# Cross-attention and FP4 feed-forward on one core: key and value projections as five one-pass products of two-part operands, key and query parts buffered for half the heads

## The chip, the cores and the metric

The kernel runs on one core of a Trainium2 chip. The metric is the device time of one launch in microseconds. The engines are TensorE (PE), VectorE (DVE), ScalarE (ACT), GpSimd (Pool) and SyncE (SP), which here only issues DMAs.

## The reference

For each of 16 batch elements, x is 512 x 256 and the context is 1601 x 192, all in float32:

```
Q = layernorm(x) @ Wq;  K = ctx @ Wk;  V = ctx @ Wv      # 16 heads of 16
P = softmax(Q K^T / 4);  x = x + (P V) @ Wo + bo
a = fp4(layernorm(x)); g = a @ fp4(w_gate)^T; u = a @ fp4(w_up)^T      # 704 wide
x = x + fp4(silu(g) * u) @ fp4(w_down)^T
```

fp4 scales blocks of 16 values by their largest magnitude, rounds to eight levels and scales back.

## The kernel before

The work of one batch element is a batch. Its 16 heads are taken in four groups of four (phases). In a group, the 1601 keys are taken in 13 tiles of 128, one step for each: four scores (keys x 512 queries, one per head), an exp of each on ACT, and a weighted sum of the four heads' values on PE. The scores have two PSUM banks in turn, so PE is at most two scores ahead of ACT.

Each projected key and query is split into three bf16 parts (`k_parts`, `q_parts`), and six pairs of parts are stacked along the contraction axis (96 rows of `k_stack`, `q_stack`), so that one bf16 matmul gives a float32-like score. The stack of one head is filled by 12 DMAs on SP's queue ("stack", g, j): six copy 16 rows of `q_parts`, six 16 rows of `k_parts`. `k_parts` and `q_parts` hold both halves of the heads (half 0: groups 0 and 1, half 1: groups 2 and 3). Three more rows carry the negated maximum of each query. It comes from the pieces: while one group is scored, PE computes the scores of the next group with the queries on the partitions, as 64 x 4 matmuls of 400 columns per batch (64 in each group), and DVE takes the maximum of each piece (L829, L1097). Then "max_parts" on DVE splits the maximum in three, "maxima" transposes it, and DMAs put it in `q_stack`.

Around this lies all other work, as events: layernorm, transposes and projections of the next batch ("ln1_*", "x_T", "ctx_T", "q_proj", "k_proj", "v_proj"), and what follows attention for the batch before, in four quarters of 128 rows ("heads_T" to "down"). A batch has 104 half-steps, 26 for each group; tables at the top (POST_AT, PRE_AT, MAX_AT, HEADS_OUT_AT, LN1) say at which half-step an event stands. `sequence` merges scores, pieces, weighted sums and rounds (PE's part of an event) into one order by estimated PE cycles; pieces go only into half-steps 0 to 21 of a group. PE, ACT and DVE follow this order, Pool and SP the order of the events. The engines take their work in that order. Rounds use two PSUM banks in turn; the engine that empties a bank counts `work_drained`, and PE waits for it.

A key or query round is two float32 products on PE (L729, L737). ACT copies it as bf16 part 0 (L867, L871), DVE subtracts that part from the bank into `rest` and frees the bank (L1003), and Pool makes parts 1 and 2 from `rest` (L1177, L1179). A context round is four transposes and a copy by ACT (L865). Values are two float32 products for each key tile (L745) and a copy by ACT (L878). At the start of a group SP issues the stacks of heads 1 to 3 of the next group, once the scores of the group before are done (they had the same slots), and the stack of head 0 of the group after it; in group 0 also x and the context of the next batch. A batch "start" (prologue) comes before the first batch; "first" prepares the feed-forward weights in the place of the post-processing, "last" prepares no batch, "tail" finishes the last one.

## Time and profile before

| | us |
|---|---|
| median of 3 runs (3776.65 to 3781.04) | 3777.42 |
| profiled execution | 3777.43 |
| its span, first to last instruction | 3775.6 |
| PE busy | 3599.6 |
| DVE busy | 2984.2 |
| ACT busy | 2242.8 |
| Pool busy | 871.0 |

The mean granted TensorE clock is 0.992. Busy time is a mean over stages with different limits. A matmul's record reaches to the end of its result, so consecutive records overlap: what one costs is read from start to start. A float32 matmul of this kernel shows as two records. The chain is the work that ended last, followed back to what released it. "SPq" rows are issues of DMAs on SP's queue.

### The profile page before, as it was taken

Reading aid. Unit: us, or ns where it says so; the run is one execution under the profiler, and the core shown is the slowest. Engines: PE = TensorE matmul, PEld = TensorE weight load, DVE = VectorE, ACT = ScalarE, POOL = GpSimd, SP = SyncE. Lnnn points to the kernel's source line nnn. Section 1 sums busy time; section 2 is a strip of 40 time slices with the busy share of each in tenths; the row PEclk is TensorE's granted clock in tenths of the full one; section 3 lists DMA queues with packets and bytes.
Section 4 is the critical chain, followed back from the end, with each engine's and each line's share of the span. In section 5 each row is a group of like instructions: output and inputs, shape, how many; then the busy total and the mean of one; then the engine's idle time right before and its main releaser. Section 6 shows DMA issues by size and latency. Waiting matters only on the chain.

```text
span 3775.6 us, 57225 instructions
## 1 busy us (share of the span) xinstructions
PE 3599.6 (95%) x19654; PEld 1643.5 (44%) x19654; DVE 2984.2 (79%) x6641; ACT 2242.8 (59%) x4350; POOL 871.0 (23%) x920
## 2 busy tenths in 40 slices
...
GB/s 67 51 50 53 24 59 34 36 54 34 51 36 42 41 42 49 29 48 39 39 55 24 60 33 35 53 36 50 35 43 40 44 49 28 49 39 38 38 22 7
DMA packets 148034, 156.44 MB, mean 41 GB/s; under 512 B 58129, under 2 KB 118818, under 8 KB 147746
## 3 DMA queue, kind: packets, MB, share of 16 engines
...
q14 instruction: 130, 1.06, 0.1%
...
## 4 chain that ended last, share of the span: by engine, by line
PE 75%; DVE 15%; ACT 4%; DMA 2%; issue 2%; SPq 1%; POOL 0%; POOLq 0%; ACTq 0%
PE out_ps L815 17%; PE score_ps L804 16%; PE piece_ps L829 16%; PE work L770 8%; DVE piece_max L1097 6%; PE work L745 5%; PE work L737 5%; PE work L780 4%; ACT probs L914 4%; DMA x_in<-in_x 2%; PE work L760 1%; PE work L724 1%; PE work L754 1%; PE work L729 1%; DVE neg_parts L1012 1%
## 5 line engine op out<-in xcount | busy, mean ns | idle before, releaser
L1097 DVE TENSOR_REDUCE piece_max<-piece_ps 128x1 f32<-128x400 f32 (+1 forms) x4096 | 2134.0, 566 | 537.3 <-PE piece_ps L829 519.5
L914 ACT ACTIVATE probs<-score_ps 128x512 f32<-128x512 f32 (+1 forms) x3328 | 1876.3, 598 | 1021.7 <-PE score_ps L804 1016.6
L829 PE MATMUL piece_ps<-k_stack,q_stack 96*128 96x400 bf16 (+1 forms) x4096 | 1282.7, 336 | 67.1 <-DVE piece_max L1097 59.5
L804 PE MATMUL score_ps<-q_stack,k_stack 99*128 99x512 bf16 (+1 forms) x3328 | 1258.5, 385 | 48.7 <-ACT probs L914 14.4
L815 PE MATMUL out_ps<-probs,v_ones 128*17 128x512 f32 x6656 | 878.0, 599 | 2.1 <-ACT probs L914 1.0
L804 PEld LDWEIGHTS score_ps<-q_stack,k_stack 99*128 99x128 bf16 (+1 forms) x3328 | 324.4, 98 | 879.7 <-ACT probs L914 642.3
L829 PEld LDWEIGHTS piece_ps<-k_stack,q_stack 96*128 96x128 bf16 x4096 | 396.8, 98 | 649.9 <-DVE piece_max L1097 430.6
L1152 POOL TENSOR_TENSOR h<-h,h_grid 128x704 f32<-128x704 f32 (+1 forms) x68 | 111.3, 1637 | 1081.7 <-DVE h_grid L966 1081.7
L770 PE MATMUL work<-wgu_T,xq_T 128*128 128x256 f32 (+1 forms) x1440 | 345.3, 361 | 0.4 <-ACT xq_T L886 0.4
L770 PEld LDWEIGHTS work<-wgu_T,xq_T 128*128 128x128 f32 x1440 | 258.8, 189 | 48.6 <-ACT xq_T L886 3.4
L815 PEld LDWEIGHTS out_ps<-probs,v_ones 128*17 128x17 f32 x6656 | 110.3, 95 | 279.7 <-issue 235.1
L737 PE MATMUL work<-ctx_T,wk_sb 128*128 128x512 f32 (+1 forms) x512 | 217.9, 513 | 0.0
L745 PE MATMUL work<-wv_sb,ctx_T 128*128 128x256 f32 (+1 forms) x832 | 215.1, 380 | 0.1
L780 PE MATMUL work<-wd_T,h_T 128*128 128x256 f32 x744 | 188.2, 378 | 0.8 <-ACT h_T L904 0.8
L1177 POOL TENSOR_TENSOR k_parts<-rest,zero 128x512 bf16<-128x512 f32 (+1 forms) x128 | 110.5, 863 | 332.5 <-DVE rest L1003 332.5
L892 ACT ACTIVATE tanh_g<-work 128x256 f32<-128x256 f32 (+1 forms) x192 | 70.4, 367 | 189.9 <-PE work L770 185.9
L745 PEld LDWEIGHTS work<-wv_sb,ctx_T 128*128 128x128 f32 (+1 forms) x832 | 151.1, 185 | 36.7 <-ACT v_ones L878 4.8
L780 PEld LDWEIGHTS work<-wd_T,h_T 128*128 128x128 f32 x744 | 137.9, 189 | 26.8 <-ACT h_T L902 1.0
L1188 POOL TENSOR_TENSOR rstd<-mean_var,eps 128x1 f32<-128x1 f32 x64 | 12.4, 193 | 475.4 <-DVE mean_var L1040 474.2
L1152 POOL TENSOR_TENSOR xq<-xq,xq_grid 128x256 f32<-128x256 f32 x60 | 43.4, 724 | 334.0 <-DVE xq_grid L966 334.0
L1179 POOL TENSOR_TENSOR k_parts<-rest,k_parts 128x512 bf16<-128x512 f32 (+1 forms) x128 | 117.7, 920 | 10.0
L871 ACT CAST k_parts<-work 128x512 bf16<-128x512 f32 (+1 forms) x128 | 63.0, 495 | 93.7 <-PE work L737 93.7
...
## 6 DMA issues: line engine op xcount, KB each, us to landing
k_stack<-k_parts SPq DMA_DIRECT2D x1536, 50.0 KB, 2.2
q_stack<-q_parts SPq DMA_DIRECT2D x1536, 16.0 KB, 1.8
...
q_stack<-neg_rows SPq DMA_DIRECT2D x192, 4.0 KB, 1.7
...
```

The costliest lines, as they stand in the source:

```text
L737: last = pe.matmul(work[:, 0:w], wk_sb[:, part, e * P:(e + 1) * P], ctx_T[:, part, a:a + w], start=(part == 0), stop=(part == 1))
L745: last = pe.matmul(work[0:r, u * D:(u + 1) * D], ctx_T[:, k, a:a + r], wv_sb[:, k, :], start=(k == 0), stop=(k == 1))
L770: last = pe.matmul(work[:, u * GW:u * GW + w], quarter(kind, t).xq_T[:, k, :], wgu_T[:, k, u, j * GW:j * GW + w], start=(k == 0), stop=(k ...
L780: last = pe.matmul(work[:, 0:D], quarter(kind, event[1]).h_T[:, c, :], wd_T[:, c, :], start=(c == 0), stop=(c == FT - 1))
L804: pe.matmul(score_ps[0:r, n % SCORE_RING, :], k_stack[:, par, slot(g, j), m * P:m * P + r], q_stack[:, par, slot(g, j), :], start=True, st ...
L815: last = pe.matmul(out_ps[32 * j:32 * j + V1, :], v_ones[0:r, batch[1] % 2, m, PER_GROUP * g + j, :], probs[0:r, step % 2, j, :], start=(m ...
L829: pe.matmul(piece_ps[:, n % PIECE_RING, 0:hi - lo], q_stack[0:SROWS, par, slot(g, j), t * P:(t + 1) * P], k_stack[0:SROWS, par, slot(g, j) ...
L914: act.activation(probs[0:r, step % 2, j, :], score_ps[0:r, (PER_GROUP * m + j) % SCORE_RING, :], ACT.Exp, scale=SCORE_SCALE).then_inc(prob ...
L1097: dve.tensor_reduce(piece_max[:, row, c:c + 1], piece_ps[:, n % PIECE_RING, 0:piece_at[c + 1] - piece_at[c]], AX_X, ALU.max).then_inc(piec ...
L1152: pool.tensor_tensor(src, src, grid, ALU.add).then_inc(done, 1)
L1177: pool.tensor_tensor(parts[:, half, 1, a:a + w], rest[:, n % 2, 0:w], zero[:].broadcast_to([P, w]), ALU.add).then_inc(split_step, 1)
L1179: pool.tensor_tensor(parts[:, half, 2, a:a + w], rest[:, n % 2, 0:w], parts[:, half, 1, a:a + w], ALU.subtract).then_inc(split_step, 1)
```

## The change

- `wk_sb`, `wv_sb` and `ctx_T` become float32r in two parts, high (a copy, rounded) and low (the float32 value less the high part). The contraction of 192 is laid out as 128 rows and 64 rows; of the context's 64 rows, the lower partitions hold the high part and the upper ones the low part. Five products (PRODUCTS) give a projection; a key round has three and two of them.
- For this the context is loaded with its last 64 columns twice (two DMAs for each chunk), the weights go through `stage_k` and `stage_v` (space of `x1`) and the events "prep_k" and "prep_v" in the prologue, and each "ctx_T" round is a copy by ACT and a subtraction by DVE.
- `k_parts` and `q_parts` hold one half of the heads. The projections of half 0 stay with the batch before, those of half 1 move to the batch itself (OWN_AT). Before the first copy of a half, ACT waits for the DMAs of the stacks that read the other half. The stacks of head 0 of groups 2 and 0 get places of their own (STACK0_AT).
- The split of a key or query round: ACT copies it twice, as part 0 and in full to `rest`; Pool subtracts, and makes parts 1 and 2.
- The two CASTs of "max_parts" become additions of zero.
- The output leaves from `x1`; `y` is gone. In the tail, `heads_T` and `xq_T` lie in `k_parts`.
- "ln2_stats", "xq_max" and "h_small" are events of their own; all tables of places and weights are new, PIECE_WEIGHT by group. Batch numbers are plain integers, with the same round numbers in effect.

```diff
+PRODUCTS = [(0, 0), (0, 1), (1, 0), (2, 2), (2, 3)]
+PRODUCT_PARTS = [(0, 1, 2), (3, 4)]
...
 POST_AT = [
-    [3, 8, 10, 11, 15, 16, 18, 21, 24, 25, 26, 29, 29, 34],
-    [24, 28, 30, 34, 36, 36, 38, 38, 41, 42, 45, 50, 52, 53],
-    [51, 56, 58, 59, 63, 64, 64, 65, 67, 70, 72, 77, 77, 82],
-    [74, 76, 78, 82, 83, 86, 86, 87, 89, 92, 92, 100, 100, 101],
+    [4, 6, 9, 10, 10, 11, 17, 19, 19, 21, 23, 24, 24, 24, 29, 29, 34],
+    [24, 26, 26, 29, 30, 33, 34, 35, 36, 36, 38, 39, 41, 46, 51, 58, 61],
+    [54, 55, 55, 58, 58, 60, 63, 66, 66, 66, 68, 68, 70, 72, 77, 82, 83],
+    [74, 75, 75, 75, 75, 82, 83, 86, 86, 88, 88, 90, 90, 92, 97, 99, 102],
 ]
 TAIL_AT = [
-    [1, 2, 3, 4, 7, 11, 11, 11, 11, 11, 11, 14, 14, 16],
-    [3, 3, 5, 7, 11, 11, 11, 11, 11, 11, 11, 14, 14, 16],
-    [5, 6, 7, 7, 11, 11, 11, 12, 13, 13, 13, 16, 16, 18],
-    [9, 9, 9, 9, 11, 12, 13, 14, 15, 15, 15, 19, 19, 20],
+    [2, 2, 2, 3, 4, 4, 6, 8, 8, 9, 9, 9, 11, 11, 14, 14, 16],
+    [3, 3, 3, 4, 5, 7, 10, 10, 11, 11, 11, 11, 12, 12, 15, 15, 18],
+    [3, 4, 6, 6, 7, 8, 11, 12, 12, 12, 12, 13, 13, 14, 16, 17, 18],
+    [6, 8, 8, 9, 9, 9, 11, 12, 14, 14, 14, 15, 15, 16, 19, 21, 22],
 ]
 
 
-PRE_AT = [9, 15, 18, 19, 24, 24, 24, 25, 32, 32, 38, 38, 38, 38, 38, 41, 46, 46, 51, 52, 57, 63, 74, 76, 79, 86, 95]
+OWN_AT = [9, 13, 14, 17, 17]
+PRE_AT = [29, 31, 31, 33, 36, 37, 40, 43, 46, 48, 48, 50, 58, 62, 67, 69, 71, 74, 80, 82, 89, 92]
+STACK0_AT = [19, 66]
 LN1 = 5
 
-HEADS_OUT_AT = 2
-MAX_AT = [22, 23]
+HEADS_OUT_AT = 1
+MAX_AT = [23, 23]
 PIECE_FROM, PIECE_TO = 0.0, 22
...
-PIECE_WEIGHT = [1.2, 1.0, 1.0, 0.9, 1.0, 1.0, 0.9, 1.0, 1.0, 1.0, 1.0, 1.0, 1.0]
-SCORE_PLACE = [0.0625, 0.2625, 0.5125, 0.7425]
-PIECE_SHIFT = 0.7
+PIECE_WEIGHT = [
+    [1.5, 1.1, 1.0, 0.5, 0.7, 0.8, 0.8, 1.0, 1.0, 0.8, 0.9, 0.5, 1.1],
+    [1.2, 1.0, 0.9, 1.0, 0.8, 0.8, 0.8, 1.2, 1.2, 1.0, 1.2, 0.7, 0.8],
+    [1.3, 1.0, 1.0, 0.5, 0.9, 1.6, 0.9, 1.0, 0.8, 1.4, 1.0, 1.0, 0.4],
+    [1.2, 0.8, 0.9, 0.7, 0.9, 0.8, 0.6, 0.6, 0.9, 0.9, 1.0, 1.3, 1.0],
+]
+SCORE_PLACE = [0.1225, 0.3525, 0.5025, 0.7525]
+PIECE_SHIFT = 0.8
...
-        names = ([("heads_T",), ("out_proj",), ("ln2_apply",), ("xq_scale",), ("xq_T",)]
+        names = ([("heads_T",), ("out_proj",), ("ln2_stats",), ("ln2_apply",), ("xq_max",), ("xq_scale",), ("xq_T",)]
                  + [("gate_up", j) for j in range(h_pieces)]
-                 + [("h_max",), ("h_scale",), ("h_grid",), ("h_T", 0), ("h_T", 1), ("down",)])
+                 + [("h_max",), ("h_small",), ("h_scale",), ("h_grid",), ("h_T", 0), ("h_T", 1), ("down",)])
...
-        loads = [("stack", (g + 1) % PHASES, j) for j in range(1, PER_GROUP)] + [("stack", (g + 2) % PHASES, 0)]
+        loads = [("stack", (g + 1) % PHASES, j) for j in range(1, PER_GROUP)] + [("stack", (g + 2) % PHASES, 0)] * (g % 2)
         if kind == "last":
             loads = loads[:3] * (g < PHASES - 1) + loads[3:] * (g < PHASES - 2)
+        if g % 2 == 0 and (g == 0 or kind != "last"):
+            put(STACK0_AT[g // 2], "stack", (g + 2) % PHASES, 0)
...
+    for h, event in zip(OWN_AT, [("q_proj", 1)] + [("k_proj", 1, c) for c in range(4)], strict=True):
+        put(h, *event)
     if kind != "last":
         pre = ([("x_T", k) for k in range(2)] + [("ctx_T", n // 2, n % 2) for n in range(8)]
-               + [("q_proj", 0)] + [("k_proj", 0, c) for c in range(4)] + [("v_proj", n) for n in range(7)]
-               + [("q_proj", 1)] + [("k_proj", 1, c) for c in range(4)])
+               + [("v_proj", n) for n in range(2)] + [("q_proj", 0)] + [("k_proj", 0, c) for c in range(4)]
+               + [("v_proj", n) for n in range(2, 7)])
...
-        k_parts = sb("k_parts", [P, 2, 3, KW], BF16)
-        q_parts = sb("q_parts", [P, 2, 3, NQ], BF16)
+        k_parts = sb("k_parts", [P, 3, KW], BF16)
+        q_parts = sb("q_parts", [P, 3, NQ], BF16)
...
+                    for to, of in ((0, 0), (C, P)):
+                        n = C - of
+                        if full:
+                            sp.dma_start(ctx_in[:, c % 2, 0:full, to:to + n],
+                                         ctx_768[nxt, a:a + full * P, of:C].rearrange("(t p) c -> p t c", p=P)).then_inc(ctx_loaded[c % 2], 16)
+                        else:
+                            sp.dma_start(ctx_in[0:w, c % 2, 0, to:to + n], ctx_768[nxt, a:a + w, of:C]).then_inc(ctx_loaded[c % 2], 16)
...
+                    w += w % 2
+                    for n in PRODUCT_PARTS[part]:
+                        of, by = PRODUCTS[n]
+                        last = pe.matmul(work[:, 0:w], wk_sb[:, by, e * P:(e + 1) * P], ctx_T[:, of, a:a + w],
+                                         start=(n == 0), stop=(n == len(PRODUCTS) - 1))
...
+                elif name in ("q_proj", "k_proj"):
+                    half = event[1]
+                    of = batch if half else nxt
+                    n, (a, w), parts = split_number(kind, event), (0, NQ), q_parts
+                    if name == "k_proj":
+                        (a, w), parts = chunk(event[2]), k_parts
+                    if kind != "start" and event in (("q_proj", half), ("k_proj", half, 0)):
+                        stacked = q_stacked if name == "q_proj" else k_stacked
+                        for par in range(2):
+                            for j in range(PER_GROUP):
+                                act.wait_ge(stacked[par][j], count(batch, 2 * KSTACKED, KSTACKED * (1 if half else 2)))
+                    act.copy(parts[:, 0, a:a + w], work[:, 0:w])
+                    if not (kind == "start" and n < 2):
+                        act.wait_ge(split_step, splits(of, n - 1, 0))
+                    act.copy(rest[:, n % 2, 0:w], work[:, 0:w]).then_inc(this_drained, 1)
...
-                    dve.wait_ge(part0_ready, count(nxt, 2 * (CHUNKS + 1), n + 1))
-                    if not (kind == "start" and n < 2):
-                        dve.wait_ge(split_step, count(nxt, 4 * (CHUNKS + 1), 2 * n - 2))
-                    dve.tensor_tensor(rest[:, n % 2, 0:w], work[:, 0:w], parts[:, half, 0, a:a + w],
-                                      ALU.subtract).then_inc(this_drained, 1)
...
+                    dve.wait_ge(ctx_hi, count(nxt, 8, 2 * c + part + 1))
+                    if part == 0:
+                        dve.tensor_tensor(ctx_T[:, 1, a:a + w], work[:, 0:w], ctx_T[:, 0, a:a + w].bitcast(F32),
+                                          ALU.subtract).then_inc(this_drained, 1)
                     else:
-                        n, (a, w), parts = split_number(kind, event), chunk(event[2]), k_parts
-                    dve.wait_ge(part0_ready, count(nxt, 2 * (CHUNKS + 1), n + 1))
-                    if not (kind == "start" and n < 2):
-                        dve.wait_ge(split_step, count(nxt, 4 * (CHUNKS + 1), 2 * n - 2))
-                    dve.tensor_tensor(rest[:, n % 2, 0:w], work[:, 0:w], parts[:, half, 0, a:a + w],
-                                      ALU.subtract).then_inc(this_drained, 1)
+                        low = ctx_T[C1:P, 2, a:a + w]
+                        dve.tensor_tensor(low, work[C1:P, 0:w], low.bitcast(F32), ALU.subtract).then_inc(this_drained, 1)
...
-                    dve.tensor_copy(neg_parts[:, 0, :], neg_max[:]).then_inc(shift_step, 1)
+                    dve.tensor_tensor(neg_parts[:, 0, :], neg_max[:], none, ALU.add).then_inc(shift_step, 1)
...
-                    pool.tensor_tensor(parts[:, half, 1, a:a + w], rest[:, n % 2, 0:w], zero[:].broadcast_to([P, w]), ALU.add).then_inc(split_step, 1)
-                    pool.wait_ge(split_step, count(nxt, 4 * (CHUNKS + 1), 2 * n + 1))
-                    pool.tensor_tensor(parts[:, half, 2, a:a + w], rest[:, n % 2, 0:w], parts[:, half, 1, a:a + w],
-                                       ALU.subtract).then_inc(split_step, 1)
+                    pool.tensor_tensor(left, left, parts[:, 0, a:a + w], ALU.subtract).then_inc(split_step, 1)
+                    pool.wait_ge(split_step, splits(of, n, 1))
+                    pool.tensor_tensor(parts[:, 1, a:a + w], left, zero[:].broadcast_to([P, w]), ALU.add).then_inc(split_step, 1)
+                    pool.wait_ge(split_step, splits(of, n, 2))
+                    pool.tensor_tensor(parts[:, 2, a:a + w], left, parts[:, 1, a:a + w], ALU.subtract).then_inc(split_step, 1)
...
-                    dve.wait_ge(y_free[t % 2], count(old, 32, 16 * (t // 2 + 1)))
-                    dve.tensor_tensor(y[:, t % 2, :], work[:, 0:D], x1[:, t, :], ALU.add).then_inc(this_drained, 1)
+                    dve.tensor_tensor(x1[:, t, :], work[:, 0:D], x1[:, t, :], ALU.add).then_inc(this_drained, 1)
```

## Rows read from the trace of the kernel before

**Rows 1.** The page: busy time of the engines; the chain by engine.

```profile
PE 3599.6 (95%) x19654; PEld 1643.5 (44%) x19654; DVE 2984.2 (79%) x6641; ACT 2242.8 (59%) x4350; POOL 871.0 (23%) x920
...
PE 75%; DVE 15%; ACT 4%; DMA 2%; issue 2%; SPq 1%; POOL 0%; POOLq 0%; ACTq 0%
```

**Rows 2.** Windows view, stages: us; busy PE, PEld, DVE, ACT, POOL; clock; DMA.

```profile
81.00:295.20 214.20, 198.45 (x1052) 71.80 (x1050) 168.60 (x361) 134.72 (x254) 53.24 (x47) 0.97 0.23 52
295.20:3500.80 3205.60, 3109.71 (x17167) 1427.75 (x17164) 2575.72 (x5754) 1955.23 (x3794) 732.21 (x770) 1.00 0.19 42
3500.80:3701.50 200.70, 186.39 (x1034) 76.09 (x1033) 142.77 (x319) 125.90 (x243) 32.57 (x33) 0.99 0.14 29
3701.50:3775.60 74.10, 51.78 (x212) 39.35 (x212) 40.72 (x106) 11.33 (x30) 30.43 (x32) 0.84 0.02 8
```

**Rows 3.** Windows view, the four head groups of batch 8.

```profile
1898.28:1950.98 52.70, 49.78 (x297) 21.40 (x300) 45.57 (x110) 34.89 (x69) 5.60 (x8) 1.00 0.28 65
1950.98:2014.24 63.26, 62.65 (x337) 31.09 (x337) 46.65 (x103) 37.56 (x76) 19.79 (x21) 1.00 0.15 29
2014.24:2072.05 57.81, 56.75 (x310) 26.02 (x314) 48.45 (x107) 34.45 (x68) 11.64 (x13) 1.00 0.16 32
2072.05:2126.61 54.56, 52.71 (x294) 23.36 (x287) 43.31 (x94) 32.73 (x64) 15.26 (x14) 1.00 0.20 45
```

**Rows 4.** Timeline, PE: start us, length us, operation, count.

```profile
1985.26 0.38 PE L804 MATMUL score_ps<-q_stack,k_stack 99*128 99x512 bf16 x1
1985.48 0.33 PE L829 MATMUL piece_ps<-k_stack,q_stack 96*128 96x400 bf16 x1
1985.65 1.02 PE L737 MATMUL work<-ctx_T,wk_sb 128*128 128x512 f32 x2
1986.51 0.33 PE L829 MATMUL piece_ps<-k_stack,q_stack 96*128 96x400 bf16 x1
...
1990.02 1.05 PE L815 MATMUL out_ps<-probs,v_ones 128*17 128x512 f32 x8
1991.00 0.39 PE L804 MATMUL score_ps<-q_stack,k_stack 99*128 99x512 bf16 x1
```

**Rows 5.** Groups by form, DVE; tile neg_parts: min/median/max ns.

```profile
L1003 DVE TENSOR_TENSOR rest<-work,k_parts 128x512 f32<-128x512 f32 x96 | 65.5, 682 | 30.7 <-ACT k_parts L871 30.6
...
L1012 DVE CAST neg_parts<-neg_max 128x16 bf16<-128x16 f32 x64 | 30.7, 480 | 2.2
...
L1012 DVE CAST neg_parts<-neg_max x64: 174/175/1379, 75.9 to 3648.7; 128x16 bf16<-128x16 f32 x64
L1014 DVE TENSOR_TENSOR neg_rest<-neg_max,neg_parts x64: 174/174/176, 76.1 to 3650.0; 128x16 f32<-128x16 f32 x64
```

**Rows 6.** Groups by form, ACT, Pool and weight loads.

```profile
L871 ACT CAST k_parts<-work 128x512 bf16<-128x512 f32 x96 | 56.3, 586 | 92.9 <-PE work L737 92.9
...
L1179 POOL TENSOR_TENSOR k_parts<-rest,k_parts 128x512 bf16<-128x512 f32 x96 | 108.0, 1125 | 7.5
...
L745 PEld LDWEIGHTS work<-wv_sb,ctx_T 128*128 128x128 f32 x768 | 142.3, 189 | 32.6 <-ACT v_ones L878 4.8 <-DVE rest L1003 0.2
```

**Rows 7.** SP's issues, group 2 of batch 8; DMA view, us to landing.

```profile
2012.55 0.53 SPq L625 DMA_DIRECT2D q_stack<-q_parts  x1
...
2034.97 0.59 SPq L625 DMA_DIRECT2D q_stack<-q_parts  x1
...
q_stack<-q_parts SPq DMA_DIRECT2D x1536, 16.0 KB, 1.8
```

**Rows 8.** Windows view, a pause of PE in batch 6 and after.

```profile
1450.00:1453.70 3.70, 2.17 (x13) 0.41 (x5) 1.94 (x10) 2.23 (x5) 0.08 (x1) 1.00 0.40 110
1453.70:1457.10 3.40, 3.04 (x8) 1.93 (x9) 3.40 (x9) 0.02 (x1) 1.14 (x2) 0.51 0.29 57
```

**Rows 9.** Timeline, start of batch 8: SP and DVE.

```profile
1897.33 0.52 SPq L625 DMA_DIRECT2D q_stack<-q_parts  x1
...
1909.24 1.41 DVE L981 BATCH_NORM_STATS2 stats<-x_in 128x6 f32<-128x256 f32 x4 [1.06 <-DMA x_in<-in_x]
```

More of the change, by code:

```diff
@@ L43 @@
 SHIFT = 3
+SPLITS = 3
 TINY = 1e-12
@@ L206, in split_number, with splits @@
         if kind == "start":
-            e = [e for e in PROLOGUE if e[0] in ("q_proj", "k_proj") and e[1] == half]
+            e = [e for e in PROLOGUE if e[0] in ("q_proj", "k_proj")]
         return (CHUNKS + 1) * half + e.index(event)
+    def splits(of, n, k):
+        return count(of, SPLITS * 2 * (CHUNKS + 1), SPLITS * n + k)
     def order(kind):
@@ L333, in count @@
     def count(batch, per, k):
-        reg, n = batch
-        return n * per + k if reg is None else reg * (2 * per) + (n * per + k)
-    def later(batch, n):
-        return batch[0], batch[1] + n
-    def at_start(batch):
-        return batch[0] is None and batch[1] == 0
-    def index(batch):
-        return count(batch, 1, 0)
+        return batch * per + k
     def round_number(kind, batch, event):
@@ L547, in resid_batch @@
         def resid_batch(kind, batch):
-            return later(batch, -1)
+            return batch - 1
         def w_view(i):
@@ L756, in fill @@
                     for k in range(2):
-                        last = pe.transpose(work[:, k * P:(k + 1) * P], heads[:, old[1] % 2, event[1], k * P:(k + 1) * P], ident[:])
+                        last = pe.transpose(work[:, k * P:(k + 1) * P], heads[:, old % 2, event[1], k * P:(k + 1) * P], ident[:])
                 elif name == "out_proj":
```

273 lines of the change are left out of this document (142 added, 131 removed).

## The prediction

> **What bounds the kernel now.** I read the busy line and the chain first. PE is busy for 95% of the span and holds 75% of the chain, DVE 15% [rows 1]. Then I cut the span into stages: up to the first exp 81 us, first batch 214.2, fourteen middle batches 3205.6 (229.0 each), last batch 200.7, tail 74.1 [rows 2]. Only the middle batches matter much, so I cut one of them (batch 8) into its four head groups: 52.7, 63.3, 57.8, 54.6 us [rows 3]. Their column for DVE says 45.6, 46.7, 48.5, 43.3: in group 0 DVE is busy for 86% of the time, though it gets no maxima pieces in the last four of 26 half-steps, and PE's busy share is the lowest there (49.8 of 52.7). Group 1 is PE's alone (62.65 of 63.26), and DVE has 26% to spare. So group 0 goes by DVE, group 1 by PE, groups 2 and 3 by both.
>
> **PE's price of the products.** The timeline gives start-to-start times [rows 4]: a bf16 score of 512 columns 0.22 us (1985.26 to 1985.48), a piece 0.17, two f32 records of 512 columns 0.86 (1985.65 to 1986.51); a value tile has four of 256, as many columns, so 0.86 too. An f32 product is two records here and each record takes twice as long per column as bf16: four passes. No float32r product is in the trace. If it runs in one pass as bf16 does, 512 columns cost 0.215 and 256 columns 0.107.
> - Key round of 512 columns: 2 x 0.86 = 1.72 becomes 5 x 0.215 = 1.08; six rounds per batch, -3.9 us. The two 65-column rounds give 0.2 at most.
> - Value tile: 0.86 becomes 5 x 0.107 = 0.54; 13 tiles, -4.2.
> - Together -8.1 to -8.3 us per batch. Bounds: every f32 weight load of 128 columns shows 189 ns [rows 6]; a 256-column product could be held to that, which costs 65 x 0.08 = 5.3 us per batch. From below I see no gain beyond one pass. I take 0.107, because a bf16 product is the nearest row. The Trainium skill (TensorE: Matmul & The Clock Gate, LDWEIGHTS) has a load as its columns over 1.2 GHz, 107 ns: the load of a value product would just keep up, and the sum would stay as it is; the row's 189 is for f32 records, so the trace neither proves nor refutes it.
>
> **DVE.** The two-part context needs a subtraction in each of the 8 context rounds; the subtraction in the 10 key and query rounds goes to Pool. One costs 682 ns at 512 columns [rows 5]: 8 long ones go, 6 come, -1.4 us per batch. The two CASTs of the maxima become TENSOR_TENSORs. The CAST takes 175 ns at the median but up to 1379, 480 on the mean; the two-input L1014 of the same size never takes over 176 [rows 5]. That is up to -0.3 us for each of 8, -2.3 us per batch. The Trainium skill (SBUF — State Buffer, SBUF: two separate sides) has DVE and GpSimd share a port pair that one of them holds for a whole instruction, and counts a DVE operation with two SBUF inputs among those that block: by that the new operations would wait as the CASTs do and the 2.3 us would stay. L1014 has two SBUF inputs and doesn't wait, so the measurement decides against it here. The 2.3 us lie in half-steps 22 to 25, where DVE has room, so I count nothing for the end either way.
>
> **ACT and Pool.** ACT copies each key and query round twice: 8 x 0.586 + 2 x 0.22 = 5.1 us per batch more [rows 6], on an engine with 34.9 of 52.7 us busy at its fullest. It follows the first copy where DVE's subtraction stood, so the bank is held no longer. Context rounds do hold their bank longer, by 0.68 us, eight times; with two banks and other work between I cost this at nothing (bound: 8 x 0.68 = 5.4). Pool gets a third operation of about 1.1 us per round [rows 6]: 10 us per batch on an engine used for 52.3 of 228.3 us. The split of a key chunk then takes 3.3 us, and the order leaves it that. Should Pool's extra work lengthen DVE's small TENSOR_SCALARs as it does the CASTs, that is 2 us per batch at most.
>
> **Where the work lies now.** I counted both event lists per group. PE's work changes by +1.5, -8.5, -1.5 and +0.3 us (the own half of the projections comes into group 0; context, first values and no more projections in group 1; a query and four key rounds in group 2). DVE's changes by about +0.5, 0, -0.3, -3.9. Group 1: 63.3 - 8.5 = 54.8, and DVE's share there rises to 46.7/54.8 = 85%, group 0's level, so that is as far as it goes. Group 0: DVE-bound, 52.7 + 1.0 = 53.7. Group 2: 56.3. Group 3: 54.6, unchanged. Sum 219.4: -8.9 us against batch 8. Bounds -12 (finer events spread DVE better) and -4 (DVE takes over earlier).
>
> **The wait that is added.** k_parts and q_parts lose one half. Before ACT may copy ("q_proj", 0) of the next batch, it waits for q_stacked of all four heads of both parities at their second load of this batch. The last of these are the DMAs of stack(3,1) to stack(3,3), which SP issues from half-step 52 on, and only when group 1's scores are done, since the slot is in use. SP takes 0.63 us per DMA: the first went out at 2012.55, the 35th, the last query part, at 2034.97, and landing takes 1.8 [rows 7]. That is 2036.8, or 22.6 us after group 2 began at 2014.2.
> When does ACT get there? The event is at half-step 58. Up to the end of the query product PE has 15 scores (3.3), 3 weighted sums of 0.98 [rows 4] (2.9), 14 pieces (2.4), an output projection (0.86), the query product (1.72) and 8 transposes (0.9, an estimate: half of a 512-column product each): 12.1 us, some 13 with PE's small gaps. So ACT stands for 22.6 - 13.0 = 9.6 us. Behind it are the exps of the next scores. PE can go on with one score, one weighted sum and two or three pieces; the next weighted sum needs the exp behind the wait. It loses what ACT loses, less what it had ahead: 9.3. DVE then runs dry too, and nothing gives this back, since group 2 has PE as its bound. And PE's clock: in batch 6 PE is busy for only 2.17 of 3.70 us, and the 3.4 us behind that have a granted clock of 0.51, the lower level of 1.2 GHz [rows 8]; a pause of 9 us will do it each time. I add 1.0 (bounds 0 and 3.4/2 = 1.7 per such stretch). Together +10.3 us per batch; bounds 0 (ACT arrives late enough) and 13.
>
> **The start of a batch.** ("down", 3) moves to half-step 102, the last step. DVE adds it only after the first piece of the next batch, and SP waits for this add, issues the output (0.6) and only then stack(1,1), x_in and the rest. Now SP starts at 1897.33, 0.95 before the batch's first exp at 1898.28, and x_in releases DVE at 1909.24 after 1.06 us of waiting [rows 9]. I put SP's start at +1.5, 2.5 later; DVE's wait grows by as much, in the group that DVE bounds. The own ("q_proj", 1) at half-step 9 waits for the query parts of stack(1,3), the 37th DMA: +1.5 + 36 x 0.63 + 1.8 = +26, where ACT would come at about +22. Part of these two waits is the same time. I take +2.5 for both; bounds 0 and 6.
>
> **The sum.** Middle batch: -8.9 + 10.3 + 2.5 = +3.9, fourteen of them +55. First batch: no post-processing, DVE -4, the same wait +10.3 and 1 at the start: +7. Last batch: its own half of the projections, 5 us of PE, comes from outside, and the start: +6. Prologue: five rounds fewer, weights to split and a longer Pool split: 0; tail: 4 quarters in a new order, -2 (bounds -8 and +5 for both). 3777.4 + 55 + 7 + 6 - 2 = 3843. The profiled execution took 3777.43 with a span of 3775.6, the median of three runs is 3777.42, so the sum stands for both.
>
> **Rivals.**
> 1. The new wait costs nothing: ACT comes late, or the queue is ahead. Then the products' gain arrives: 14 x -8.9, first -4, last +5, -2: 3652. Against: the 0.63 us per DMA stands in each row. For: the margin is one number, the place of half-step 58, and PE 98% busy in groups 1 and 2 shows how evenly the order runs now. The turning point is a wait of 8.9 us in total per batch; above it the change loses. Chance 0.27.
> 2. The waits are there but smaller, 5 to 8 us per batch, and the new order saves more than the count: 3700 to 3765, faster all the same. 0.09.
> 3. Gain and wait cancel: 3777. 0.07.
> 4. Weight loads show: 65 products per batch at 189 ns, +5.3 x 16 = +85: 3928. 0.05.
> 5. The change doesn't do what it says: float32r takes four passes. 21.7 us per batch become 54: some +500. 0.02; nothing in the trace speaks for it.
>
> **How the numbers follow.** The forecast (3843, its own range 3795 to 3885) has 0.50. A measurement of this kernel can't tell 0.2%, 7.6 us, from no change. Faster is rivals 1 and 2: 0.36; within 0.2% rival 3: 0.07; slower the forecast with 4 and 5: 0.57. The range runs from 3645 (most of rival 1) to 3890.
>
> **What would show it.** In the profile after: L737 and L745 records of one pass, 215 and 107 ns start to start (rival 5 and 4 otherwise). ACT idle before the query parts' copy in group 2 for 9 to 10 us, released by a DMA, in 15 batches; PE's clock at half right after it; group 2 at 66 us where group 1 is near 55. DVE waiting 3 us or more for x_in. The neg_parts operations at 175 ns throughout. The forecast is wrong if group 2 takes under 60 us, or if groups 0 and 1 together fall under 103.

## The result and the profile after

The changed kernel takes 4045.84 us (median of 4 runs, 4028.89 to 4052.26), the kernel before beside it 3777.03. The ratio is 1.0704, 95% interval [1.0676, 1.0733]: slower by 7.0%, where I had forecast 1.7%. The profiled execution took 4028.89 us with a span of 4027.0; it is the shortest of the four, so what is read from the trace explains some 17 us less than the median shows.

The page of the changed kernel: busy lines, the chain by engine and by line, and the row of one ACT copy (busy, mean ns of one | idle before it and who ended it). L896 is ACT's copy of a projection into its parts, L636 and L637 are SP's issues of query and key parts.

```profile
PE 3560.1 (88%) x19990; PEld 1686.2 (42%) x19990; DVE 3020.4 (75%) x6616; ACT 2308.1 (57%) x4514; POOL 1038.7 (26%) x1078
...
PE 57%; SPq 19%; DVE 12%; ACT 3%; DMA 3%; issue 3%; POOL 2%; ACTq 0%; POOLq 0%; DVEq 0%
...
L896 ACT CAST q_parts<-work 128x512 bf16<-128x512 f32 x32 | 18.8, 586 | 263.3 <-DMA q_stack<-q_parts 261.4
```

PE's share fell from 95 to 88%, and SP's queue went from 1 to 19% of the chain [rows 1]. One operation of 0.6 us, done 32 times, has 261 us of idle time ahead of it, ended by a DMA: about as much as the whole loss of 269 us, in one row. What the clock costs behind these waits and what the products gain come on top of it, with opposite signs.

The windows view, stages of the changed kernel (us; busy PE, PEld, DVE, ACT, POOL; clock; DMA), to be laid beside [rows 2]:

```profile
82.60:323.20 240.60, 201.72 (x1074) 75.38 (x1072) 169.49 (x360) 138.44 (x265) 63.30 (x57) 0.90 0.21 48
323.20:3755.90 3432.70, 3074.32 (x17459) 1465.02 (x17458) 2608.20 (x5726) 2011.09 (x3934) 879.99 (x910) 0.95 0.19 41
```

A middle batch takes 3432.7/14 = 245.2 us where it took 229.0; the last batch takes 204.7, the tail 66.4. The same view of batch 8 by head group, to be laid beside [rows 3]:

```profile
2038.08:2098.60 60.52, 53.00 (x285) 22.67 (x284) 46.82 (x110) 35.72 (x71) 18.47 (x23) 0.94 0.23 54
2098.60:2154.90 56.30, 54.62 (x332) 27.05 (x330) 48.20 (x106) 37.29 (x74) 11.90 (x11) 1.00 0.20 43
2154.90:2228.20 73.30, 57.98 (x315) 27.89 (x315) 49.46 (x106) 36.76 (x74) 23.35 (x25) 0.91 0.13 25
2228.20:2284.00 55.80, 55.14 (x320) 27.73 (x319) 41.93 (x90) 34.10 (x65) 9.14 (x7) 0.97 0.19 43
```

Group 1 gained 7 us, group 0 lost 7.8, group 2 lost 15.5, and these two have a granted clock of 0.94 and 0.91 where it had been 1.00. The timeline of ACT in the same batch shows the two places (start, length, operation, [idle before, releaser]):

```profile
2061.82 0.59 ACT L896 CAST q_parts<-work 128x512 bf16<-128x512 f32 x1 [6.06 <-DMA q_stack<-q_parts]
...
2165.98 1.09 ACT L942 ACTIVATE probs<-score_ps 128x512 f32<-128x512 f32 x2 [0.48 <-PE score_ps L817]
2177.86 0.59 ACT L896 CAST q_parts<-work 128x512 bf16<-128x512 f32 x1 [10.79 <-DMA q_stack<-q_parts]
```

ACT ends its exps at 2167.07 and stands until 2177.86: 12.2 us into group 2 it arrives, at 23.0 the DMAs let it go (forecast 13.0 and 22.6). The other stand is 17.7 to 23.7 us into group 0. PE and SP around the second one; L817 is a score, L828 the weighted sum:

```profile
2168.68 0.38 PE L817 MATMUL score_ps<-q_stack,k_stack 99*128 99x512 bf16 x1
2179.49 1.91 PE L828 MATMUL out_ps<-probs,v_ones 128*17 128x512 f32 x8 [10.43 <-ACT probs L942]
```

```profile
2153.93 0.53 SPq L636 DMA_DIRECT2D q_stack<-q_parts  x1
...
2175.93 0.59 SPq L636 DMA_DIRECT2D q_stack<-q_parts  x1
```

From 2153.93 to 2175.93 SP issues query and key parts in turn, one each 0.63 us, and the last query part is the one that ACT waits for. The weighted sum behind the pause takes 1.91 us where it takes 1.05 otherwise. What the pause leaves behind, in windows of PE before, in and after it:

```profile
2166.00:2168.90 2.90, 2.90 (x16) 0.73 (x14) 1.61 (x5) 1.07 (x2) 0.00 (x0) 1.00 0.25 47
2168.90:2179.50 10.60, 0.17 (x3) 0.01 (x2) 1.78 (x5) 1.64 (x4) 0.49 (x1) 0.64 0.26 50
2179.50:2182.50 3.00, 3.00 (x12) 0.85 (x13) 0.62 (x2) 0.43 (x1) 2.84 (x4) 0.50 0.00 0
2182.50:2185.50 3.00, 3.00 (x9) 1.97 (x8) 1.07 (x3) 0.99 (x2) 2.05 (x4) 0.51 0.00 0
2185.50:2188.50 3.00, 3.00 (x16) 2.19 (x16) 2.07 (x5) 0.91 (x3) 0.00 (x0) 1.00 0.00 0
```

PE was busy without a gap before, then idle for 10.4 of 10.6 us, and then it has work all the time but the lower level, 1.2 GHz, for 6 us: 3 us lost behind the pause.

### The profile page after: what moved, and what is told of

It reads as the page before. It is cut to its first block, busy times and chain, and to the rows that moved or that the text cites. A ratio compares the mean times of both kernels' runs of the same rounds, so it can differ in the third digit from the quotient of the medians.

```text
span 4027.0 us, 58280 instructions
## 1 busy us (share of the span) xinstructions
PE 3560.1 (88%) x19990; PEld 1686.2 (42%) x19990; DVE 3020.4 (75%) x6616; ACT 2308.1 (57%) x4514; POOL 1038.7 (26%) x1078
## 4 chain that ended last, share of the span: by engine, by line
PE 57%; SPq 19%; DVE 12%; ACT 3%; DMA 3%; issue 3%; POOL 2%; ACTq 0%; POOLq 0%; DVEq 0%
PE piece_ps L842 13%; PE out_ps L828 13%; PE score_ps L817 12%; SPq L636 9%; SPq L637 9%; PE work L783 7%; DVE piece_max L1143 7%; PE work L793 4%; PE work L749 3%; PE work L757 2%; ACT probs L942 2%; DMA q_stack<-neg_rows 1%; DMA q_stack<-q_parts 1%; SPq L644 1%; POOL k_parts L1226 1%
## 5 line engine op out<-in xcount | busy, mean ns | idle before, releaser
L817 PE MATMUL score_ps<-q_stack,k_stack 99*128 99x512 bf16 (+1 forms) x3328 | 1280.3, 393 | 173.2 <-ACT probs L942 109.5
L842 PE MATMUL piece_ps<-k_stack,q_stack 96*128 96x400 bf16 (+1 forms) x4096 | 1313.9, 345 | 50.4 <-DVE piece_max L1143 28.4
L828 PE MATMUL out_ps<-probs,v_ones 128*17 128x512 f32 x6656 | 906.0, 617 | 150.4 <-ACT probs L942 148.7
L817 PEld LDWEIGHTS score_ps<-q_stack,k_stack 99*128 99x128 bf16 (+1 forms) x3328 | 327.5, 100 | 826.9 <-ACT probs L942 584.2
L828 PEld LDWEIGHTS out_ps<-probs,v_ones 128*17 128x17 f32 x6656 | 111.1, 96 | 438.6 <-issue 223.9
L1224 POOL TENSOR_TENSOR rest<-rest,k_parts 128x512 f32<-128x512 f32 (+1 forms) x128 | 121.3, 948 | 353.7 <-ACT rest L899 353.7
L793 PE MATMUL work<-wd_T,h_T 128*128 128x256 f32 x744 | 202.5, 397 | 0.8 <-ACT h_T L932 0.8
L749 PE MATMUL work<-ctx_T,wk_sb 128*128 128x512 f32 (+1 forms) x640 | 198.7, 421 | 2.3 <-DVE ctx_T L1035 2.3
L757 PE MATMUL work<-wv_sb,ctx_T 128*128 128x256 f32 (+1 forms) x1040 | 189.2, 317 | 4.5 <-DVE wv_sb L1029 4.4
L896 ACT CAST q_parts<-work 128x512 bf16<-128x512 f32 x32 | 18.8, 586 | 263.3 <-DMA q_stack<-q_parts 261.4
L749 PEld LDWEIGHTS work<-ctx_T,wk_sb 128*128 128x128 f32 x640 | 117.4, 195 | 28.2 <-issue 3.5
L1226 POOL TENSOR_TENSOR k_parts<-rest,zero 128x512 bf16<-128x512 f32 (+1 forms) x128 | 120.8, 943 | 10.0
```

Of the source, the lines that this page charges most:

```text
L749: last = pe.matmul(work[:, 0:w], wk_sb[:, by, e * P:(e + 1) * P], ctx_T[:, of, a:a + w], start=(n == 0), stop=(n == len(PRODUCTS) - 1))
L757: last = pe.matmul(work[0:r, u * D:(u + 1) * D], ctx_T[:, of, a:a + r], wv_sb[:, by, :], start=(n == 0), stop=(n == len(PRODUCTS) - 1))
L793: last = pe.matmul(work[:, 0:D], quarter(kind, event[1]).h_T[:, c, :], wd_T[:, c, :], start=(c == 0), stop=(c == FT - 1))
L817: pe.matmul(score_ps[0:r, n % SCORE_RING, :], k_stack[:, par, slot(g, j), m * P:m * P + r], q_stack[:, par, slot(g, j), :], start=True, st ...
L828: last = pe.matmul(out_ps[32 * j:32 * j + V1, :], v_ones[0:r, batch % 2, m, PER_GROUP * g + j, :], probs[0:r, step % 2, j, :], start=(m == ...
L842: pe.matmul(piece_ps[:, n % PIECE_RING, 0:hi - lo], q_stack[0:SROWS, par, slot(g, j), t * P:(t + 1) * P], k_stack[0:SROWS, par, slot(g, j) ...
```

## The experiments

All times are medians; the ratio to the kernel before is from runs on the same chip. "Groups" are the four head groups of batch 8 from the windows view.

**1. The query projection of the next batch later** (half-step 58 to 64, its key round 62 to 66):

```diff
-PRE_AT = [29, 31, 31, 33, 36, 37, 40, 43, 46, 48, 48, 50, 58, 62, 67, 69, 71, 74, 80, 82, 89, 92]
+PRE_AT = [29, 31, 31, 33, 36, 37, 40, 43, 46, 48, 48, 50, 64, 66, 67, 69, 71, 74, 80, 82, 89, 92]
```

> Only the places of the next batch's query and key rounds in group 2 change: half-steps 58, 62 become 64, 66. Theory A (ACT's wait for the query parts' DMAs, and PE's clock after it, make the loss): the wait of 10.6 us in group 2 goes, with some 3 us that PE loses at half clock after it; 15 x 13 = some 200 us less than the changed kernel's 4029 profiled, so 3820 to 3860. Rival B (the loss is in the order and the amount of work; the wait only takes time that would be lost anyway): under 60 us less.

Measured 3864.88 us, ratio 1.0230 [1.0215, 1.0246], 181 us under the changed kernel and 5 above the range of Theory A. Its group 2:

```profile
2062.80:2123.10 60.30, 55.48 (x315) 26.77 (x315) 49.47 (x106) 36.72 (x74) 23.35 (x25) 1.00 0.15 31
```

Group 2 went from 73.3 to 60.3: 13.0 us for a pause of 10.4. So a pause costs its length and some 2.6 us of clock. (Group 3 took 57.3 us for 55.8, so over the whole batch it is 12.5 us.) ACT's wait fell from 261.4 to 101.1 us in total; what is left is the one in group 0.

**2. All three places** (experiment 1, the own query projection at half-step 13, down at 100):

```diff
-OWN_AT = [9, 13, 14, 17, 17]
+OWN_AT = [13, 13, 14, 17, 17]
...
-    [74, 75, 75, 75, 75, 82, 83, 86, 86, 88, 88, 90, 90, 92, 97, 99, 102],
+    [74, 75, 75, 75, 75, 82, 83, 86, 86, 88, 88, 90, 90, 92, 97, 99, 100],
```

> The places in group 2 as 64 and 66, the own query round from half-step 9 to 13, the last quarter's down from 102 to 100. Theory A: both waits go, with the half clock behind them, and SP starts a batch 2 us earlier: 15 x (13.6 + 8.8 + 1.5) = some 360 us less than 4029: 3650 to 3700, faster than the kernel before (3777). Rival B: over 3900.

Measured 3808.37 us, ratio 1.0077 [1.0060, 1.0094]: no ACT wait for the query stacks is left at all, group 0 is 55.6 us for the 59.5 of experiment 1, and the kernel is still not faster than before, where I had expected 3650 to 3700. So the waits for the query parts aren't the whole story. Group 3 took 57.6 us, and PE stands for 2.9 us at the end of group 2 and 1.2 at the end of group 3, released by the DMA that puts the maxima (neg_rows) into the query stack: 49 such waits, 68.0 us in all. In the kernel before they were 4, of 5.9 us in all; in the changed kernel 36, of 52.5.

**3. No wait for the query parts: two buffers for them.** Only the query side gets both halves back; the keys keep one.

```diff
-        q_parts = sb("q_parts", [P, 3, NQ], BF16)
+        q_parts = sb("q_parts", [P, 2, 3, NQ], BF16)
...
-act.wait_ge(stacked[par][j], count(batch, 2 * KSTACKED, KSTACKED * (1 if half else 2)))
+act.wait_ge(stacked[par][j], count(batch, 2 * KSTACKED, KSTACKED * ((1 if half else 2) - (name == "q_proj"))))
```

> q_parts holds both halves again (3 KB per partition more), and ACT waits for no query stack; all places stay, the wait for the key parts stays. Theory A: the waits of 10.6 us (group 2) and 5.8 us (group 0) go and leave what the key parts' DMAs then ask at the first key round, 2 to 3 us each; 15 x (8 + 3 + 3 + 2) = some 240 us less: 3770 to 3830. Rival B: under 60 us less. Rival C (what counts is the last DMA of a stack, query or key alike): the first key round waits as long as the query round did, under 100 us less.

Measured 3766.88 us, ratio 0.9965 [0.9953, 0.9976]. The wait for the query parts is worth 279 us, all of the loss and 10 us more; from one load of x to the next, a middle batch falls from 245.4 to 227.2. ACT waits for the key parts instead, but only 19.1 us in all. Its groups:

```profile
1900.30:1954.00 53.70, 50.71 (x286) 21.91 (x284) 46.68 (x110) 35.51 (x71) 18.60 (x23) 1.00 0.26 61
1954.00:2010.30 56.30, 54.59 (x332) 26.99 (x330) 48.20 (x106) 37.20 (x73) 11.91 (x11) 1.00 0.20 43
2010.30:2071.80 61.50, 55.58 (x315) 26.75 (x315) 50.85 (x106) 36.70 (x75) 23.45 (x25) 0.99 0.15 30
2071.80:2129.00 57.20, 56.54 (x321) 27.70 (x319) 41.95 (x90) 34.16 (x66) 9.14 (x7) 0.95 0.19 43
```

These test my count of the work without the wait (53.7, 54.8, 56.3, 54.6): group 0 is right, group 1 is 1.5 us too long, group 2 5.2, and group 3 2.6, at a clock of 0.95. What is late there is seen on SP (the timeline; L644 carries the maxima):

```profile
2067.28 0.59 SPq L637 DMA_DIRECT2D k_stack<-k_parts  x1
2067.91 2.07 SPq L644 DMA_DIRECT2D q_stack<-neg_rows  x3
...
2071.15 0.61 PE L817 MATMUL score_ps<-q_stack,k_stack 99*128 99x512 bf16 x1 [2.85 <-DMA q_stack<-neg_rows]
```

The 12 DMAs for head 0 of the next batch wait for the last key chunk, which Pool ends at 2059.50, and the maxima, which PE needs at once, are queued behind them: ACT has them ready at 2065.11, and SP issues them at 2067.91. PE stands for 2.85 us and goes on at half clock (that score takes 0.61 for 0.38, and the granted clock is 0.50 up to 2077).

**4. The same waits, another order of DMAs.** On the changed kernel, SP issues the query parts of heads 2 and 3 before the key parts of head 2 (the cut shows the new loop alone; the old places of these issues are left out for heads 2 and 3):

```diff
+                    if j == 2:
+                        for jj in (2, 3):
+                            for n in range(len(STACK)):
+                                put_q(jj, n)
```

> Nothing changes but the order of SP's issues at the start of a group: the twelve query DMAs of heads 2 and 3 go ahead of their key DMAs, so that the last query part is read 12 x 0.63 = 7.6 us earlier. Theory A: the wait in group 2 falls from 10.6 to 3 us, that in group 0 from 5.8 to nothing; the first key round then waits 2 to 3 us. Some 200 to 240 us less: 3790 to 3830. Rival B: under 60 us less. A theory in which ACT's place alone decides, and not the queue, expects no change.

Measured 3823.85 us, ratio 1.0119 [1.0104, 1.0134], 222 us under the changed kernel, with every event in its place. The wait in group 0 is gone (53.0 us), that in group 2 is at most 4.4 us (60.7 in 15 waits), and group 2 takes 66.1. It is the place of a DMA in SP's queue that sets when ACT may go on: the last query part is now the 24th DMA of the group and not the 35th (11 places, not the 12 that I expected), 11 x 0.63 = 6.9 us, and ACT's stand in group 2 fell by 7.2, from 10.8 to 3.6.

**5. The keys earlier,** on top of experiment 3, so that head 0's parts are ready and sent before the maxima are due:

```diff
-PRE_AT = [29, 31, 31, 33, 36, 37, 40, 43, 46, 48, 48, 50, 58, 62, 67, 69, 71, 74, 80, 82, 89, 92]
+PRE_AT = [29, 31, 31, 33, 36, 37, 40, 43, 46, 48, 48, 50, 58, 62, 64, 66, 69, 74, 80, 82, 89, 92]
```

> On q_double (3767): the next batch's key rounds from half-steps 62, 67, 69, 71 to 62, 64, 66, 69, so that Pool has split them 4 us earlier and SP has issued stack(0,0) before the negated maxima of group 3 are ready. Theory A (SP's queue also makes the 3.0 us pause of PE at the end of group 2, with a stretch of half clock behind it): 15 x 4 = 60 us less, 3700 to 3730. Rival (that pause comes from the chain of the maxima on DVE alone): no change.

Measured 3694.87 us, ratio 0.9777 [0.9763, 0.9792]: faster than both kernels. Its groups 2 and 3, and SP and PE at the same place:

```profile
1972.60:2032.20 59.60, 55.47 (x316) 26.79 (x316) 49.99 (x106) 37.05 (x75) 22.50 (x25) 1.00 0.16 31
2032.20:2086.40 54.20, 53.54 (x321) 26.77 (x319) 41.67 (x90) 33.89 (x66) 9.14 (x7) 1.00 0.20 45
```

```profile
2024.59 0.59 SPq L637 DMA_DIRECT2D k_stack<-k_parts  x1
2027.74 2.83 SPq L644 DMA_DIRECT2D q_stack<-neg_rows  x3
...
2031.74 0.39 PE L817 MATMUL score_ps<-q_stack,k_stack 99*128 99x512 bf16 x1 [0.84 <-DMA q_stack<-neg_rows]
```

The queue is empty 2.5 us before the maxima. PE waits 0.84 us for 2.85, its clock stays up, and groups 2 and 3 take 4.9 us less: 2.0 us of pause and 2.9 of clock. 72 us in all, where 60 were expected.

**6. The maxima one half-step earlier,** on top of 5:

```diff
-MAX_AT = [23, 23]
+MAX_AT = [22, 23]
```

> On keys_earlier: max_parts one half-step before maxima again (22 and 23 instead of 23 and 23). PE waits 45 us in all for neg_parts in q_double, 0.85 us in groups 0 and 1 and 1.7 in group 2. Theory A: two thirds of that goes, 25 to 45 us less than keys_earlier. Rival: DVE's other work takes the room, within 10 us.

Measured 3697.95 us, ratio 0.9789 [0.9774, 0.9803]: no different from 5, where Theory A had 25 to 45 us less. PE's wait for the sums of the maxima fell only from 45.1 to 35.4 us. This kernel is the base of experiments 7 to 9.

**7. Four-pass products back:** f32 operands, two products instead of five, all else as in 6.

```diff
-PRODUCTS = [(0, 0), (0, 1), (1, 0), (2, 2), (2, 3)]
-PRODUCT_PARTS = [(0, 1, 2), (3, 4)]
+PRODUCTS = [(0, 0), (2, 2)]
+PRODUCT_PARTS = [(0,), (1,)]
...
-        wk_sb = sb("wk_sb", [P, 4, D], F32R)
+        wk_sb = sb("wk_sb", [P, 4, D], F32)
```

(`wv_sb` and `ctx_T` likewise; it leaves out the low parts' products.)

> On maxima_chain: context, key and value weights in float32 instead of float32r, two four-pass products in the place of the five one-pass ones; order, splits and all else as they are. Theory: the five products show 234 and 118 ns each, so the change of products is worth 6 x (1.72 - 1.17) + 13 x (0.86 - 0.59) = 6.8 us of PE per batch; if PE is the bound there, this kernel is 100 to 110 us slower than maxima_chain. Rival (DVE or the exps are the bound by now): under 50 us slower.

Measured 3782.06 us, ratio 1.0009 [0.9999, 1.0019]. The five products are worth 3782.06 - 3697.95 = 84 us, 5.3 per batch, under the 100 to 110 expected. All the rest of the change together (order, context subtraction, ACT's and Pool's extra operations), with the query parts in two buffers and the maxima's DMAs in time, takes as long as the kernel before; what the order is worth by itself, no run shows. The price of a product is read in the timeline of the changed kernel, from start to start at full clock:

```profile
2188.00 1.05 PE L749 MATMUL work<-ctx_T,wk_sb 128*128 128x512 f32 x3
2188.89 0.52 PE L842 MATMUL piece_ps<-k_stack,q_stack 96*128 96x400 bf16 x2
...
2146.39 0.38 PE L817 MATMUL score_ps<-q_stack,k_stack 99*128 99x512 bf16 x1
2146.42 0.94 PE L757 MATMUL work<-wv_sb,ctx_T 128*128 128x256 f32 x5
2147.20 0.39 PE L817 MATMUL score_ps<-q_stack,k_stack 99*128 99x512 bf16 x1
```

The weight loads of ten of the value products there (ns, min/median/max):

```profile
L757 PEld LDWEIGHTS work<-wv_sb,ctx_T x10: 187/190/202, 2146.4 to 2147.8; 128*128 128x128 f32 x10
```

From one score to the next, 0.81 us: less 0.22 for the score [rows 4], 0.59 for five products of 256 columns, 0.118 each. Of 512 columns three take 0.92 (from the score at 2187.97) less 0.22, 0.233 each. The weight loads last 190 ns and don't hold the products to that pace.

**8. The maxima's two operations as copies again,** on top of 6:

```diff
-dve.tensor_tensor(neg_parts[:, 0, :], neg_max[:], none, ALU.add)
+dve.tensor_copy(neg_parts[:, 0, :], neg_max[:])
```

> e10_maxima_chain with the two type conversions of the maxima (L1050, L1054) written as copies again, as in the kernel before; nothing else differs. Theory A (the lock, not the form of the operation, makes these operations long: they stand at 175 ns alone and up to 1.7 us beside a Pool operation, in either form; e10 shows L1050 266, L1052 503, L1054 443, L1056 409 ns on the mean, the kernel before had 480, 175, 443, 175): the four sum up to 80 to 105 us again, none of it sets the end for more than 0.3 us a batch, 3693 to 3703 us. Rival B (a copy on DVE's two ports waits longer than a sum does and PE's maxima transposes come later): 3710 to 3730. Rival C (a copy is free of the lock): L1052 and L1056 alone stay long, 3690 or less.

Measured 3696.34 us, ratio 0.9784 [0.9767, 0.9800]: the same as 6. The groups of DVE in it (copies at L1050 and L1054, sums at L1052 and L1056):

```profile
L1052 DVE TENSOR_TENSOR neg_rest<-neg_max,neg_parts 128x16 f32<-128x16 f32 x64 | 32.2, 502 | 2.2
L1054 DVE CAST neg_parts<-neg_rest 128x16 bf16<-128x16 f32 x64 | 28.3, 443 | 2.2
...
L1050 DVE CAST neg_parts<-neg_max 128x16 bf16<-128x16 f32 x64 | 20.7, 324 | 2.2
```

With sums, experiment 6 has 322 ns for L1050 and 443 for L1054, and 502 for L1052 as here. (The 266 that I gave as its L1050 is that of experiment 5.) Both forms are held up alike. Theory A stands.

**9. Pool's rounding of h out of the maxima's way,** on top of 6:

```diff
-    [54, 55, 55, 58, 58, 60, 63, 66, 66, 66, 68, 68, 70, 72, 77, 82, 83],
+    [54, 55, 55, 58, 58, 60, 63, 66, 66, 66, 68, 68, 70, 76, 80, 82, 84],
```

> On maxima_chain: the third quarter's h_grid, whose three Pool operations of 1.4 to 1.7 us lie beside max_parts in group 2, goes from half-step 72 to 76, h_T and down three later. Theory P (a DVE operation with two SBUF inputs stands while Pool's operation runs, whether CAST or TENSOR_TENSOR): the neg_parts and neg_rest operations in group 2 fall from up to 1674 ns to 175, PE's 1.7 us pause there goes; 15 to 40 us less than maxima_chain. Rival: they stay long, since Pool isn't the cause.

Measured 3776.37 us, ratio 0.9995 [0.9985, 1.0004]: 78 us slower than 6, which I hadn't expected. First the maxima's chain in 6, with Pool beside it, then in 9:

```profile
2028.25 1.68 POOL L1201 TENSOR_TENSOR h<-h,h_grid 128x704 f32<-128x704 f32 x1
2028.35 1.61 DVE L1052 TENSOR_TENSOR neg_rest<-neg_max,neg_parts 128x16 f32<-128x16 f32 x1
2029.99 0.17 DVE L1054 TENSOR_TENSOR neg_parts<-neg_rest,zero 128x16 bf16<-128x16 f32 x1
2030.01 1.41 POOL L1204 TENSOR_TENSOR h<-h,h_small 128x704 f32<-128x704 f32 x1
2030.20 1.25 DVE L1056 TENSOR_TENSOR neg_parts<-neg_rest,neg_parts 128x16 bf16<-128x16 f32 x1
```

```profile
2062.66 0.18 DVE L1052 TENSOR_TENSOR neg_rest<-neg_max,neg_parts 128x16 f32<-128x16 f32 x1
2063.08 0.17 DVE L1056 TENSOR_TENSOR neg_parts<-neg_rest,neg_parts 128x16 bf16<-128x16 f32 x1
...
2074.06 1.38 POOL L1204 TENSOR_TENSOR h<-h,h_small 128x704 f32<-128x704 f32 x1
2075.59 1.09 PE L790 MATMUL work<-ident,h 128*128 128x128 f32 x4 [3.13 <-POOL h L1204]
```

And group 3 of 9:

```profile
2068.80:2130.70 61.90, 57.77 (x325) 28.81 (x323) 43.45 (x95) 34.92 (x66) 13.87 (x10) 0.94 0.17 40
```

In this group nothing holds the four operations any more (175 ns each; over all groups L1052 has a mean of 187 ns for 502 and L1056 175 for 409, L1050 and L1054 still 305 and 427), group 2 is 56.7 us for 58.7, but PE now reaches h's transposes before Pool has ended: 3.13 us of pause, then 5.9 us at a granted clock of 0.50 with PE busy throughout, and group 3 takes 61.9 us at a clock of 0.94.

**10. The transposes two places later as well:**

```diff
-    [54, 55, 55, 58, 58, 60, 63, 66, 66, 66, 68, 68, 70, 76, 80, 82, 84],
+    [54, 55, 55, 58, 58, 60, 63, 66, 66, 66, 68, 68, 70, 76, 82, 84, 85],
```

> e13_pool_away with h's transposes two places later too (h_grid 76, h_T0 82, h_T1 84, down 85 in the third group). In e13 of batch 8 the four operations of the maxima chain took 175 ns each with Pool quiet (in e10 up to 1.6 us), PE came to the maxima's transpose 2.0 us earlier, and group 2 was 56.8 us for 58.7; but Pool ended h's rounding at 173.3 us of the batch where PE wanted it at 170.0: 3.3 us of pause, then TensorE at half clock, and group 3 was 61.9 us for 54.2. Theory A (a pause of 3 us costs 8 because of the clock; nothing else is wrong with e13): with the transposes at about 174 the pause is gone, group 2 56.8, group 3 54 to 55, 2 us a batch under e10's 3697.95: 3665 to 3685, granted clock 0.99. Rival B (down one or two places later holds up the group's start, or v_proj's products behind it): 3700 to 3740, the pause moved into group 3's first steps at another line. Rival C (the pause isn't what costs): 3770 as e13.

Measured 3690.93 us, ratio 0.9770 [0.9755, 0.9784]; forecast 3665 to 3685. Group 2 takes 56.9 us; group 3:

```profile
2030.40:2085.70 55.30, 54.48 (x325) 27.06 (x323) 42.98 (x95) 34.67 (x66) 13.89 (x10) 1.00 0.20 44
```

Group 3 fell by 6.6 us with a pause of 3.1: Theory A holds for the pause. The 1.8 us that group 2 gained on experiment 6 were kept only in part, since group 3 takes 55.3 for 54.2: work pushed out of one group stands in the next. The forecast had it at 54 to 55 with the whole gain kept. This version has the lowest time of the study, 7 us (0.2%) under 6 and 4 under 5, differences that a measurement of this kernel can't tell from none.

## Why the prediction was wrong

The sign and the mechanism were right: the products gain, and the added ACT wait eats it all. The size was not: forecast +66 us, measured +269. What failed are sizes in the sum of a middle batch (+3.9 forecast, +16.2 measured): the clock behind a pause, the start of a batch, and the work without the wait. In the profiled execution the middle batches gave 14 x (245.2 - 232.9) = +172 over the forecast, the first batch +19, the last -2, prologue and tail together -4; that is the 186 between 3843 and the profiled execution. By group, batch 8 stands so against the forecast: group 0 60.5 for 53.7 + 2.5, group 1 56.3 for 54.8, group 2 73.3 for 56.3 + 10.3, group 3 55.8 for 54.6. Of the 6.7 us over in group 2, 4.0 are there without the wait too (60.3 in experiment 1 for 56.3), and 2.7 are pause and clock (13.0 for 10.3). The steps:

- **The wait in group 2: right.** I put ACT's stand at 9.6 us, it is 10.8 in batch 8 (arrival 0.8 early, release 0.4 late); experiments 1 and 3 take it away and 4 shortens it, in three ways, and the time falls each time.
- **The clock behind a pause: the first mis-sized term.** I had added 1.0 us for it, with 1.7 as its bound, from one stretch of 3.4 us at half clock after a pause of 1.5 us [rows 8]. After the 10.4 us pause it was 6 us at half clock, 3.0 lost; three pairs of runs give 2.6 (experiment 1), 2.9 (5) and 3.5 (10) beyond the pause itself. I had taken one short stretch for the upper end. Short stretches do occur: in group 0 of experiment 1 a pause of 6.1 us is followed by 2.5 us at 0.50 and 3.0 at 0.84, 1.7 us lost by an estimate from these two windows. And I charged it once per batch, where it falls due two or three times (clock 0.94, 0.91 and 0.97 in groups 0, 2 and 3).
- **The start of a batch: the second.** I put +2.5 for SP's later start and the own wait at half-step 9 together, bounds 0 and 6. Group 0 took 60.5 us for 53.7 without the wait (experiment 3): +6.8, above the upper bound. ACT came to that copy at 17.7 us and not at 22, and the DMAs let it go at 23.7 (26 forecast): a wait of 6 us, not of 4, with half clock behind it (0.50 for 5.3 us), which the term had left out. The other half of that term, DVE waiting for x_in, did not come: its statistics row has 6.9 us of idle time in 64 operations in all, less than the 28.8 of the kernel before.
- **The work without the wait: the third.** Groups of 53.7, 54.8, 56.3, 54.6 were forecast; experiment 3 has 53.7, 56.3, 61.5, 57.2. The count by engine saw what PE, DVE and ACT do, and not SP: the maxima's DMAs had got behind the 12 of head 0's new place. I had asked what else stands in SP's queue for the start of the batch alone. With this cleared (experiments 5 and 10) the four groups sum up to 222.9 and 222.5, against 219.4 forecast. Of what remains in group 2 of experiment 5, 1.5 us is PE's wait for the maxima's sums on DVE, see below.
- **The products: a size.** 8.1 to 8.3 us per batch forecast. By start-to-start times it is 6 x (1.72 - 1.17) + 13 x (0.86 - 0.59) = 6.8, for a float32r column costs 0.46 ns and not bf16's 0.42; in time it came to 5.3 (experiment 7). PE was busy for 5.8 us less in batch 8 there; that DVE, busy for 85% of groups 0 and 1, holds the rest back is possible, but no run tested it. Rival 4, weight loads that show, would have had 189 ns between the products and is refuted by the 118 measured: the record of such a load still shows 187 to 202 ns, not 107, and the products don't keep to it. The 118 refute rival 5, float32r in four passes, too.
- **The maxima's operations: wrong.** I expected 175 ns throughout. The four groups of the changed kernel take 104.4 us, more than the 81.5 of the kernel before. Its own timeline had the reason, and I had read only a minimum, a median and a maximum of it (kernel before, DVE and Pool, batch 8):

```profile
2062.07 1.67 POOL L1154 TENSOR_TENSOR h<-h,h_grid 128x704 f32<-128x704 f32 x1
2062.39 1.38 DVE L1012 CAST neg_parts<-neg_max 128x16 bf16<-128x16 f32 x1
2063.80 0.17 DVE L1014 TENSOR_TENSOR neg_rest<-neg_max,neg_parts 128x16 f32<-128x16 f32 x1
2063.82 1.41 POOL L1157 TENSOR_TENSOR h<-h,h_small 128x704 f32<-128x704 f32 x1
2064.01 1.25 DVE L1016 CAST neg_parts<-neg_rest 128x16 bf16<-128x16 f32 x1
```

L1012 ends with the Pool operation beside it, L1014 slips into the gap before the next, L1016 ends with that one. In this batch L1014 isn't slow because its turn comes when Pool has just ended, not because a sum with two inputs is free. The Trainium skill (SBUF — State Buffer, SBUF: two separate sides) has such operations among those that a Pool instruction blocks; I decided against it on that one row, and experiments 6 and 9 show it right (L1052 1.61 us beside Pool, 0.18 without). Nor was it right that the end doesn't feel these operations: PE's wait for the last of them is 44.7 us in the changed kernel, 17.3 in the kernel before (where they stood one half-step earlier), and without Pool beside them group 2 took 2.0 us less (experiment 9). In the time of the whole kernel experiment 10 got back 7 us at most.

Why it adds up as it does: rival 1, the waits cost nothing, was put at 3652. With the products at 84 us for 8.2 x 16 = 131 it is 3699, and the kernel without the query wait and with the maxima's DMAs in time (experiment 5) measured 3694.87. So the account closes as a sum; by group it doesn't, and there errors cancel: 52.8, 56.3, 59.6 and 54.2 us in experiment 5 for 53.7, 54.8, 56.3 and 54.6. Not settled: how the 279 us of the query wait divide between its pauses and their clock, since experiments 1 and 2 move work besides the wait, and 4 moves DMAs.
